# Group attention: the low part of the probabilities two slots behind the scores, four probability buffers, and the half product ahead of the jobs in each slot

## The chip, the cores and the metric

The kernel runs on one core of one Trainium2 chip, in one launch. The metric is the device time of a run in microseconds (us); the kernel before takes 2767.14 us, the median of three runs (2764.65 to 2774.29).

## The reference, cut to what matters

One decoder layer on x of shape (2, 512, 512): causal self-attention with 16 heads, then a grouped attention, then an expert layer with 8 experts. Each adds to x after a layer norm. The change lies in the second part:

```python
q  = _ln(fp8_linear(ln_out, wq)  ...)          # 8 groups x 2 heads, head size 128
k  = _ln(fp8_linear(ln_out, wk)  ...); v = fp8_linear(ln_out, wv)
core = softmax(q  @ k.T  / sqrt(128)) @ v      # 512 keys: x itself
qx = _ln(fp8_linear(ln_out, wqx) ...)
xout = softmax(qx @ kx.T / sqrt(128)) @ vx     # 1024 keys: the context
catq = to_fp8(concat([core, xout]) / proj_smooth)
x = x + (catq @ wproj.T) * (proj_in_scale * proj_w_scale)
```

The output has to agree with a float32 computation, so a float32 operand of a matrix product is kept as two float16 parts, high and low, and a product is three matmuls: high by high, high by low, low by high.

## The kernel before, in words

The group attention (`group_attention`, lines 1189 to 1691) works through 16 steps, one for each of 8 groups and 2 batches (`STEPS`). A step has 16 slots, numbered u = 0 to 15. A slot is one block of 128 queries by all keys of one kind. Slots 0 to 7 are self slots (two heads, four blocks each, 512 keys, scores of 128x512); slots 8 to 15 are cross slots (1024 keys, 128x1024). The steps are written out for the first and the last group, and are the body of a hardware loop over the six groups between: two steps in each pass.

Every engine has a queue of its own, written out slot by slot, and waits on counters (semaphores) that the others raise. For unit u (the work that begins in slot u) the chain is:

- TensorE, `scores`: three or six matmuls into one of two PSUM buffers, `SC[u % 2]`. It waits until the exponential of unit u-2 has read that buffer.
- VectorE, `maxima` (line 1513): the negated row maximum.
- ScalarE, `exp` (line 1430): exp(score - max) into `prob[u % 2]`, float32, with its row sum. It waits for the maximum, and until `parts_lo` of unit u-2 has read the buffer.
- VectorE, `reciprocal` (lines 1517 and 1519): the factor from the row sum of unit u-1, in slot u.
- ScalarE, `parts_hi` (line 1438): prob times the factor, as float16, of unit u-1, in slot u, right after the exponential of unit u.
- VectorE, `parts_lo` (line 1525): prob times the factor minus the high part, as float16. Before, this is unit u-1 in slot u, and the last thing VectorE does in the slot.
- SyncE, `turn` (line 1278): a DMA transpose of both parts into `pt[u % 8]`.
- TensorE, `product`: values times turned probabilities of a pair of units, in two halves. It runs LAG = 6 slots behind: in slot u, the half number u % 2 of the pair that begins with unit u-6 (or u-7). The first half waits until both units of the pair have landed.

Beside this chain a slot has jobs (`SLOT_JOBS`): A0 to A3 (slots 0 to 3) and B0, B1 (4, 5) project queries, keys and values of the next step; Y0 to Y3 (8 to 11) are the output projection of the step before; T4 (12), T0 (13), T1 (14), T2 and T3 (15) turn the normalised queries and keys of the next step. TensorE runs the job after `scores` and, before the change, ahead of `product`. ScalarE reads an A, B or T job at the end of the same slot (`read_job`), after `exp` and `parts_hi`. VectorE takes up what the job gives in the next slot. Jobs use two PSUM banks by turns, and a job waits until the one before it in its bank has been read: T1 for T4, T3 for T1.

An output of attention is read by ScalarE (`output`, line 1446, in slots 2, 6, 10, 14), rounded to float8 by VectorE in four short operations (`output_round`, lines 850 to 856, in slots 3, 6, 11, 15) and finished by GpSimd (`quantised`, line 1348, into `cat`). The job Y0 waits for all four kinds of the step before; the last of them is read and rounded in slot 6 and finished in slot 7. GpSimd also splits the weights of coming groups (lines 1297 to 1304) and, from slot 7, normalises the queries and keys that the T jobs turn (lines 1316 to 1333).

Of the kernel before, what the change touches and what calls it, by code (L numbers as in the profile page):

```python
# [15 lines left out]
ALU = mybir.AluOpType  # L16
ACT = mybir.ActivationFunctionType
AX = mybir.AxisListType
F32 = mybir.dt.float32
# [5 lines left out]
P = 128  # L25
B, S, D = 2, 512, 512
# [40 lines left out]
def after(eng, sem, count):  # L67

    if not isinstance(count, int) or count > 0:
        eng.wait_ge(sem, count)  # L70
# [754 lines left out]
SX = 1024  # L825
# [4 lines left out]
UX = KINDS * BT  # L830
SELF_U = HPG * BT
SLOTS = 8
PARTS_KEPT = 4
LAG = 6
P_SCALE = 2.0 ** 15
# [348 lines left out]
def landings(n, u):  # L1184

    return 16 * (UX // SLOTS * n + u // SLOTS + 1)


def group_attention(nc, ins, sem, sb, bank, X, ident, cols, rcols, xq, kv_d, gw, rows3):


# [4 lines left out]
    STEPS = GROUPS * B  # L1196
# [11 lines left out]
    kv = [sb(f"xkv{b}", [P, KV], F16) for b in range(B)]  # L1208
    kxh, kxl = ([kv[b][:, SX * i:SX * (i + 1)] for b in range(B)] for i in range(2))
    vxh, vxl = ([kv[b][:, SX * i:SX * (i + 1)].rearrange("p (t c) -> p t c", t=XT) for b in range(B)] for i in (2, 3))  # L1210
    prob = [sb(f"xprob{i}", [P, SX], F32) for i in range(2)]
    parts = [sb(f"xparts{i}", [P, 2 * SX], F16) for i in range(PARTS_KEPT)]
    pt = sb("xpt", [P, SLOTS, 2 * XT, P], F16)
    nm, rs, ri = (sb(f"x{x}", [P, 4], F32) for x in ("nm", "rs", "ri"))
    rr = sb("xrr", [P, 1], F32)
    hcols = sb("hcols", [P, 8], F32)
    y, unit, total = sb("xy", [P, S], BF16), sb("xunit", [P, S], BF16), sb("xtotal", [P, S], BF16)
    cat = sb("cat", [P, KINDS, S], F16)
# [2 lines left out]
    SC = [bank[:, 2 * i:2 * i + 2, :].rearrange("p a c -> p (a c)") for i in range(2)]  # L1221
# [47 lines left out]
    with nc.Block() as block:  # L1269
# [115 lines left out]
        def _(act):  # L1385
# [40 lines left out]
            def exp(n, u):  # L1426
                L = S if u < SELF_U else SX
                act.wait_ge(maxed, UX * n + u + 1)
                after(act, lo, UX * n + u - 1)
                act.activation(prob[u % 2][:, 0:L], SC[u % 2][:, 0:L], ACT.Exp,  # L1430
                               bias=nm[:, u % 4:u % 4 + 1], accum_out=rs[:, u % 4:u % 4 + 1]).then_inc(exped, 1)

            def parts_hi(n, u):

                L = S if u < SELF_U else SX
                act.wait_ge(recip, UX * n + u + 1)
                after(act, landed[(u - PARTS_KEPT) % SLOTS], landings(n, u - PARTS_KEPT))
                act.activation(parts[u % PARTS_KEPT][:, 0:L], prob[u % 2][:, 0:L], ACT.Copy,  # L1438
                               scale=ri[:, u % 4:u % 4 + 1]).then_inc(hi, 1)

            def output(n, kind):
# [44 lines left out]
        def _(dve):  # L1486
# [27 lines left out]

            def reciprocal(n, u):
                dve.wait_ge(exped, UX * n + u + 1)
                dve.reciprocal(rr[:], rs[:, u % 4:u % 4 + 1]).then_inc(inverted, 1)
                dve.wait_ge(inverted, UX * n + u + 1)
                dve.tensor_scalar(ri[:, u % 4:u % 4 + 1], rr[:], P_SCALE, None, ALU.mult).then_inc(recip, 1)  # L1519

            def parts_lo(n, u):
                L = S if u < SELF_U else SX
                dve.wait_ge(hi, UX * n + u + 1)
                part = parts[u % PARTS_KEPT]
                dve.scalar_tensor_tensor(out=part[:, L:2 * L], in0=prob[u % 2][:, 0:L],  # L1525
                                         scalar=ri[:, u % 4:u % 4 + 1], in1=part[:, 0:L], op0=ALU.mult,
                                         op1=ALU.subtract).then_inc(lo, 1)

# [24 lines left out]
            def step(g, n, b, first, last, last_group):  # L1553
                for u in range(UX):
                    maxima(n, u)
                    if not (first and u == 0):
                        reciprocal(n if u else n - 1, (u - 1) % UX)
                    for name in SLOT_JOBS.get(u - 1, ()):
                        if name[0] == "Y" and not first:
                            project_out(n - 1, int(name[1]), 1 - b)  # L1560
                        if name in V_ORDER and not last:
                            value_lo(name, n + 1, 1 - b)
                        if name[0] in "AB" and not last:
                            block_stats(name, n + 1)
                    if u in ROUND_AT and not (first and u < LAG + 2):
                        output_round(n if u >= LAG + 2 else n - 1, ROUND_AT[u])
                    if u == 7 and b == 0:

                        after(dve, o_read, KINDS * n)
                        dve.tensor_copy(rsm[:], rcols[:, bass.ds(C_SMOOTH + KINDS * g, KINDS)]).then_inc(s_rsm, 1)  # L1570
                    if not (first and u == 0):
                        parts_lo(n if u else n - 1, (u - 1) % UX)

            def body(g, first, last):
                step(g, 2 * g, 0, first, False, last)
# [1 line left out]

            loop(body)(dve)
            reciprocal(STEPS - 1, UX - 1)
            parts_lo(STEPS - 1, UX - 1)  # L1580
            output_round(STEPS - 1, 2)
            output_round(STEPS - 1, 3)
# [6 lines left out]
        def _(pe):  # L1589
# [44 lines left out]
            def scores(n, u, b):  # L1634
                kind, qt = u // BT, u % BT
                after(pe, exped, UX * n + u - 1)
                tok = slice(P * qt, P * (qt + 1))
                q, l = qh[b][:, kind, tok], ql[b][:, kind, tok]
                a, c = (kh[b], kl[b]) if u < SELF_U else (kxh[b], kxl[b])
                for j in range(1 if u < SELF_U else 2):  # L1640
                    r = slice(S * j, S * (j + 1))
                    last = three(pe, SC[u % 2][:, r], q, l, a[:, r], c[:, r], True, True)
                last.then_inc(scored, 1)
# [23 lines left out]
            def step(g, n, b, first, first_before, last):  # L1667
                for u in range(UX):
                    if u % BT == 0:
                        pe.wait_ge(t_lo, len(T_ORDER) * n + 2 + u // BT)  # L1670
                    if u == SELF_U:
                        pe.wait_ge(kv_in[b], 16 * (g + 1))
                    scores(n, u, b)
                    for name in SLOT_JOBS.get(u, ()):
                        if name in jobs_of(first, last):
                            if b == 1 and name == "A0":
                                pe.wait_ge(w_lo, w_base(g) + W1N)
                            if b == 1 and name == "B0":
                                pe.wait_ge(w_lo, w_base(g) + W1N + W2N)
                            if b == 1 and name == "Y0":  # L1680
                                pe.wait_ge(w_lo, w_base(g) + (W3N if last else WN))
                            run_job(name, n + 1, 1 - b, jobs_of(first, last), NEXT if first else jobs_of(first_before, False))
                    if not (first and u < LAG):
                        product(n if u >= LAG else n - 1, (u - LAG) % UX // 2, b if u >= LAG else 1 - b, u % 2)

            def body(g, first, last):
                step(g, 2 * g, 0, first, False, False)
# [313 lines left out]
```

## Time and profile before

| | us |
|---|---|
| median of three runs | 2767.14 (2764.65 to 2774.29) |
| the profiled execution | 2769.0 |
| its span, first to last instruction | 2767.2 |
| TensorE matmuls busy | 2398.0 (87%) |
| VectorE busy | 1413.4 (51%) |
| ScalarE busy | 1124.9 (41%) |
| GpSimd busy | 1138.1 (41%) |

The mean granted TensorE clock is 0.930 of full speed. A line of a timeline gives the start and length of an instruction or of several alike, its engine, its line in the kernel, its operation, the tiles that it writes and reads, their shapes and count, and in brackets how long the engine had been idle before it and for whom it waited. Matmuls are pipelined: one can be shown as running while the next has begun, so the time that one takes is the distance between two starts. The group attention lies between about 563 and 1745 us of the span; the expert layer follows.

### The profile page before, as it was taken

The numbers are of one execution on the slowest core, as the hardware profiler recorded it, in microseconds if no ns is written. First come the engines' busy times: TensorE is split into PE (matmuls) and PEld (weight loads), VectorE is DVE, ScalarE is ACT, GpSimd is POOL, SyncE is SP. The second block draws the span as 40 slices with busy tenths as digits, with TensorE's granted clock in tenths as the row PEclk, the third lists the DMA queues.
The fourth block names the chain that finished last, engine by engine and source line by source line (L and its number), as shares of the span: only waits on it lengthen the run. The fifth ranks groups of instructions, "written<-read, shape, count | busy, mean of one in ns | idle before, by whom it ended". The sixth has DMA issues, their size and how long they took to land. (4 is left out here: it accounts for less than half of the span.)

```text
span 2767.2 us, 42142 instructions
## 1 busy us (share of the span) xinstructions
PE 2398.0 (87%) x14528; PEld 1338.6 (48%) x14528; DVE 1413.4 (51%) x2920; ACT 1124.9 (41%) x2101; POOL 1138.1 (41%) x1476
## 2 busy tenths in 40 slices
PE   6899899768877878788878876699999999999999
PEld 4566444435555555455545543344444444444444
DVE  5766784347776767676767765522222122322221
ACT  3455464456665656565556653211111111111110
POOL 3322266476565646464637450332231313132231
PEclk9899799889998989898989998799999999999999
DMA  3100022245656566666566564302011110102000
GB/s 136 44 17 5 16 92 107 92 107 107 145 107 133 108 130 112 108 122 125 118 124 122 107 126 80 152 31 92 31 61 53 38 61 30 61 30 91 0 0 30
DMA packets 421584, 225.03 MB, mean 81 GB/s; under 512 B 404400, under 2 KB 404912, under 8 KB 413232
## 3 DMA queue, kind: packets, MB, share of 16 engines
q1 hardware_dynamic: 415952, 186.74, 29.5%
q10 hardware_dynamic: 5472, 36.18, 3.8%
q8 instruction: 97, 1.59, 0.2%
q14 instruction: 63, 0.52, 0.1%
HBM read 103.34 MB, written 18.87 MB: 44 GB/s over the span
## 5 line engine op out<-in xcount | busy, mean ns | idle before, releaser
L1430 ACT ACTIVATE xprob<-bank,xnm 128x512 f32<-128x512 f32 (+1 forms) x256 | 230.7, 901 | 460.4 <-DVE xnm L1513 460.3
L1525 DVE SCALAR_TENSOR_TENSOR xparts<-xprob,xri,xparts 128x512 f16<-128x512 f32 (+1 forms) x256 | 288.5, 1127 | 238.3 <-ACT xparts L1438 237.6
L1804 ACT ACTIVATE sil<-bank 128x512 f32<-128x512 f32 x128 | 76.4, 597 | 772.4 <-PE bank L299 772.4
L1777 POOL TENSOR_SCALAR hh<-h 128x512 f16<-128x512 f32 x128 | 105.1, 821 | 679.0 <-DVE h L1875 678.8
L1875 DVE TENSOR_TENSOR h<-bank,sil 128x512 f32<-128x512 f32 x128 | 88.6, 692 | 530.6 <-PE bank L299 423.2
L1513 DVE TENSOR_REDUCE xnm<-bank 128x1 f32<-128x512 f32 (+1 forms) x256 | 243.6, 952 | 95.5 <-PE bank L299 94.6
L1438 ACT ACTIVATE xparts<-xprob,xri 128x512 f16<-128x512 f32 (+1 forms) x256 | 236.3, 923 | 1.9 <-DVE xri L1519 1.9
L297 PE MATMUL bank<-eXTh,ewh_gate 128*128 128x512 f16 x512 | 194.8, 380 | 4.3 <-DVE ewl_gate L1822 4.3
L298 PE MATMUL bank<-eXTh,ewl_gate 128*128 128x512 f16 x512 | 194.6, 380 | 0.0
L299 PE MATMUL bank<-eXTl,ewh_gate 128*128 128x512 f16 x512 | 194.6, 380 | 0.0
L297 PE MATMUL bank<-eXTh,ewh_up 128*128 128x512 f16 x512 | 194.1, 379 | 0.3 <-DVE ewl_up L1822 0.3
L298 PE MATMUL bank<-eXTh,ewl_up 128*128 128x512 f16 x512 | 194.0, 379 | 0.0
L299 PE MATMUL bank<-eXTl,ewh_up 128*128 128x512 f16 x512 | 194.0, 379 | 0.0
L297 PE MATMUL bank<-ewh_down,hh 128*128 128x512 f16 x512 | 194.0, 379 | 0.0
L298 PE MATMUL bank<-ewh_down,hl 128*128 128x512 f16 x512 | 194.0, 379 | 0.0
L299 PE MATMUL bank<-ewl_down,hh 128*128 128x512 f16 x512 | 194.0, 379 | 0.0
L1625 PE MATMUL bank<-ident,qr 128*128 128x128 f32 x320 | 63.2, 330 | 140.7 <-ACT ft L1423 83.7
L1348 POOL TENSOR_TENSOR cat<-xtotal,xunit 128x512 f16<-128x512 bf16 x64 | 84.0, 1312 | 234.7 <-DVE xtotal L856 234.7
L1333 POOL TENSOR_SCALAR qr<-qr,xrstd,xshift 128x128 f32<-128x128 f32 x320 | 168.9, 545 | 3.1 <-POOL xshift L1328 2.7
L1779 POOL TENSOR_TENSOR hl<-h,hh 128x512 f16<-128x512 f32 x128 | 153.3, 1198 | 21.9 <-POOL hh L1777 20.5
L297 PE MATMUL bank<-xpt,xkv 128*128 128x256 f16 x512 | 151.5, 296 | 9.5 <-DMA xpt<-xparts 9.5
L1630 PE MATMUL bank<-xw3h,cat 128*128 128x512 f16 x256 | 106.6, 416 | 60.9 <-POOL cat L1348 57.2
(259 smaller groups left out, 6034.2 us busy)
## 6 DMA issues: line engine op xcount, KB each, us to landing
xkv<-kv_made ACTq DMA_DIRECT2D x16, 1024.0 KB, 6.5
raw_gate<-in_gate SPq DMA_DIRECT2D x8, 2048.0 KB, 8.0
raw_up<-in_up SPq DMA_DIRECT2D x8, 2048.0 KB, 8.0
raw_down<-in_down SPq DMA_DIRECT2D x8, 2048.0 KB, 8.1
xwraw<-in_w_group ACTq DMA_DIRECT2D x15, 1024.0 KB, 5.2
kv_made<-vst SPq DMA_DIRECT2D x16, 512.0 KB, 4.2
kv_made<-kst SPq DMA_DIRECT2D x16, 512.0 KB, 2.6
kvraw<-in_w_kvx SPq DMA_DIRECT2D x4, 1024.0 KB, 6.5
```

The source lines that it names most:

```text
L297: pe.matmul(ps, ah, bh, start=start, stop=False)
L298: pe.matmul(ps, al, bh, start=False, stop=False)
L299: return pe.matmul(ps, ah, bl, start=False, stop=stop)
L1333: pool.tensor_scalar(norm_block(i), norm_block(i), rstd[:, i:i + 1], shift[:, i:i + 1], ALU.mult, ALU.add)\
L1430: act.activation(prob[u % 2][:, 0:L], SC[u % 2][:, 0:L], ACT.Exp, bias=nm[:, u % 4:u % 4 + 1], accum_out=rs[:, u % 4:u % 4 + 1]).then_inc( ...
L1438: act.activation(parts[u % PARTS_KEPT][:, 0:L], prob[u % 2][:, 0:L], ACT.Copy, scale=ri[:, u % 4:u % 4 + 1]).then_inc(hi, 1)
L1513: dve.tensor_reduce(nm[:, s:s + 1], SC[u % 2][:, 0:L], AX.X, ALU.max, negate=True).then_inc(maxed, 1)
L1525: dve.scalar_tensor_tensor(out=part[:, L:2 * L], in0=prob[u % 2][:, 0:L], scalar=ri[:, u % 4:u % 4 + 1], in1=part[:, 0:L], op0=ALU.mult, o ...
L1630: pe.matmul(J, c, w3h[:, kind, :], start=(kind == 0), stop=False)
L1777: pool.tensor_scalar(hh[half][:, f, :], h[i % 2][:], 1.0, 1.0, ALU.mult, ALU.mult).then_inc(h_hi, 1)
L1779: pool.tensor_tensor(hl[half][:, f, :], h[i % 2][:], hh[half][:, f, :], ALU.subtract).then_inc(h_lo, 1)
L1875: dve.tensor_tensor(h[i % 2][:], bank[:, 2 * (i % 2) + 1, :], sil[i % 2][:], ALU.mult).then_inc(made, 1)
```

## The change: what it does

`parts_lo` of unit u-2, not u-1, runs in slot u, and its place in VectorE's queue is right after `reciprocal`, ahead of the jobs and the rounding. The exponential of unit u would then overwrite a buffer still to be read, so there are four probability buffers and not two: three of 1024 columns that units 1 to 15 take in turn, and one of 512 columns for unit 0. The exponential of unit u waits for `parts_lo` of the unit that had its buffer before: u-3 for u above 3, and units 13, 14, 15 of the step before for u = 1, 2, 3. The reciprocal's scratch gets four columns. On TensorE `product` moves ahead of the jobs in each slot.

```diff
+def prob_of(u):
+    return (u - 1) % 3 if u else 3
+
+def prob_user(u):
+    return u - 3 if u > 3 else u - 4 if u else -UX
...
-    prob = [sb(f"xprob{i}", [P, SX], F32) for i in range(2)]
+    prob = [sb(f"xprob{i}", [P, SX], F32) for i in range(3)] + [sb("xprob_s", [P, S], F32)]
...
-                after(act, lo, UX * n + u - 1)
-                act.activation(prob[u % 2][:, 0:L], SC[u % 2][:, 0:L], ACT.Exp,
+                after(act, lo, UX * n + prob_user(u) + 1)
+                act.activation(prob[prob_of(u)][:, 0:L], SC[u % 2][:, 0:L], ACT.Exp,
...
                     maxima(n, u)
                     if not (first and u == 0):
                         reciprocal(n if u else n - 1, (u - 1) % UX)
+                    if not (first and u < 2):
+                        parts_lo(n if u >= 2 else n - 1, (u - 2) % UX)
                     for name in SLOT_JOBS.get(u - 1, ()):
...
-                    if not (first and u == 0):
-                        parts_lo(n if u else n - 1, (u - 1) % UX)
...
             reciprocal(STEPS - 1, UX - 1)
+            parts_lo(STEPS - 1, UX - 2)
             parts_lo(STEPS - 1, UX - 1)
...
                     scores(n, u, b)
+                    if not (first and u < LAG):
+                        product(n if u >= LAG else n - 1, (u - LAG) % UX // 2, b if u >= LAG else 1 - b, u % 2)
                     for name in SLOT_JOBS.get(u, ()):
...
-                    if not (first and u < LAG):
-                        product(n if u >= LAG else n - 1, (u - LAG) % UX // 2, b if u >= LAG else 1 - b, u % 2)
```

## Rows read from the trace of the kernel before

**Rows 1.** Busy times: page; middle steps (PE, PEld, DVE, ACT, POOL, clock, DMA share, GB/s).
```profile
PE 2398.0 (87%) x14528; PEld 1338.6 (48%) x14528; DVE 1413.4 (51%) x2920; ACT 1124.9 (41%) x2101; POOL 1138.1 (41%) x1476
...
637.90:1644.10 1006.20, 802.99 (x5546) 532.61 (x5545) 704.27 (x1492) 594.63 (x1038) 566.95 (x811) 0.91 0.61 120
```

**Rows 2.** Timeline of VectorE, cross slots 11 to 13 of step 7.
```profile
1114.60 0.28 DVE L850 TENSOR_SCALAR xy<-xy 128x512 bf16<-128x512 bf16 x1
...
1116.08 1.28 DVE L1525 SCALAR_TENSOR_TENSOR xparts<-xprob,xri,xparts 128x1024 f16<-128x1024 f32 x1
1117.28 1.22 DVE L1513 TENSOR_REDUCE xnm<-bank 128x1 f32<-128x1024 f32 x1
...
1118.67 0.74 DVE L1507 SCALAR_TENSOR_TENSOR X<-bank,psc,X 128x512 f32<-128x512 f32 x1
1120.81 1.28 DVE L1525 SCALAR_TENSOR_TENSOR xparts<-xprob,xri,xparts 128x1024 f16<-128x1024 f32 x1 [1.40 <-ACT xparts L1438]
1122.01 1.22 DVE L1513 TENSOR_REDUCE xnm<-bank 128x1 f32<-128x1024 f32 x1
```

**Rows 3.** Timeline of ScalarE, slots 12 and 14 of step 7.
```profile
1118.53 1.11 ACT L1430 ACTIVATE xprob<-bank,xnm 128x1024 f32<-128x1024 f32 x1 [2.49 <-DVE xnm L1513]
...
1119.64 1.14 ACT L1438 ACTIVATE xparts<-xprob,xri 128x1024 f16<-128x1024 f32 x1
1120.67 0.77 ACT L1421 ACTIVATE xkh<-bank,hcols 128x512 f16<-128x512 f32 x1
1121.34 0.77 ACT L1423 ACTIVATE ft<-bank,hcols 128x512 f32<-128x512 f32 x1
...
1130.13 0.68 ACT L1446 ACTIVATE xy<-bank,rsm 128x512 bf16<-128x512 f32 x1
```

**Rows 4.** Timeline of TensorE, cross slots 9 and 15 of step 7.
```profile
1104.90 0.38 PE L297 MATMUL bank<-xkv,xqh 128*128 128x512 f16 x1
...
1106.20 0.38 PE L1630 MATMUL bank<-xw3h,cat 128*128 128x512 f16 x1
...
1107.92 0.27 PE L297 MATMUL bank<-xpt,xvh 128*128 128x256 f16 x1
...
1108.58 0.38 PE L297 MATMUL bank<-xkv,xqh 128*128 128x512 f16 x1
...
1132.27 1.11 PE L1625 MATMUL bank<-ident,qr 128*128 128x128 f32 x4 [4.65 <-ACT ft L1423]
```

**Rows 5.** Timeline of TensorE, self slots 1 and 2 of step 8: starts of scores.
```profile
1146.66 0.38 PE L297 MATMUL bank<-xkh,xqh 128*128 128x512 f16 x1
...
1150.37 0.38 PE L297 MATMUL bank<-xkh,xqh 128*128 128x512 f16 x1
```

**Rows 6.** Timeline of VectorE: slots 6 and 9 of step 8, slot 0 of step 9.
```profile
1166.11 0.69 DVE L1513 TENSOR_REDUCE xnm<-bank 128x1 f32<-128x512 f32 x1 [0.42 <-PE bank L299]
...
1168.84 0.52 DVE L850 TENSOR_SCALAR xy<-xy 128x512 bf16<-128x512 bf16 x1 [0.96 <-ACT xy L1446]
...
1180.73 1.23 DVE L1513 TENSOR_REDUCE xnm<-bank 128x1 f32<-128x1024 f32 x1 [1.32 <-PE bank L299]
...
1214.66 0.69 DVE L1513 TENSOR_REDUCE xnm<-bank 128x1 f32<-128x512 f32 x1 [0.52 <-PE bank L299]
```

**Rows 7.** Timeline of GpSimd and of TensorE, slots 7 and 8 of step 8.
```profile
1172.31 1.49 POOL L1348 TENSOR_TENSOR cat<-xtotal,xunit 128x512 f16<-128x512 bf16 x1 [0.79 <-DVE xtotal L856]
...
1173.94 0.58 PE L1630 MATMUL bank<-xw3h,cat 128*128 128x512 f16 x1 [4.62 <-POOL cat L1348]
```

**Rows 8.** Timeline of TensorE: first scores of step 8, first in a pass of the loop.
```profile
1140.30 0.61 PE L297 MATMUL bank<-xkh,xqh 128*128 128x512 f16 x1 [4.50 <-issue]
```

**Rows 9.** The tile xpt: DMA transposes, from issue to landing.
```profile
DMA to landing us min/median/max: 3.0/4.2/9.5
```

**Rows 10.** Timeline of VectorE: a low part of 512 columns while GpSimd splits weights.
```profile
1086.76 1.74 DVE L1525 SCALAR_TENSOR_TENSOR xparts<-xprob,xri,xparts 128x512 f16<-128x512 f32 x1 [0.38 <-ACT xparts L1438]
...
1090.55 0.75 DVE L1525 SCALAR_TENSOR_TENSOR xparts<-xprob,xri,xparts 128x512 f16<-128x512 f32 x1 [0.38 <-ACT xparts L1438]
```

More of the change, by code:

```diff
@@ L1210, in group_attention @@
     vxh, vxl = ([kv[b][:, SX * i:SX * (i + 1)].rearrange("p (t c) -> p t c", t=XT) for b in range(B)] for i in (2, 3))
-    prob = [sb(f"xprob{i}", [P, SX], F32) for i in range(2)]
+    prob = [sb(f"xprob{i}", [P, SX], F32) for i in range(3)] + [sb("xprob_s", [P, S], F32)]
     parts = [sb(f"xparts{i}", [P, 2 * SX], F16) for i in range(PARTS_KEPT)]
     pt = sb("xpt", [P, SLOTS, 2 * XT, P], F16)
-    nm, rs, ri = (sb(f"x{x}", [P, 4], F32) for x in ("nm", "rs", "ri"))
-    rr = sb("xrr", [P, 1], F32)
+    nm, rs, rr, ri = (sb(f"x{x}", [P, 4], F32) for x in ("nm", "rs", "rr", "ri"))
     hcols = sb("hcols", [P, 8], F32)
@@ L1437, in parts_hi @@
                 after(act, landed[(u - PARTS_KEPT) % SLOTS], landings(n, u - PARTS_KEPT))
-                act.activation(parts[u % PARTS_KEPT][:, 0:L], prob[u % 2][:, 0:L], ACT.Copy,
+                act.activation(parts[u % PARTS_KEPT][:, 0:L], prob[prob_of(u)][:, 0:L], ACT.Copy,
                                scale=ri[:, u % 4:u % 4 + 1]).then_inc(hi, 1)
@@ L1516, in reciprocal @@
                 dve.wait_ge(exped, UX * n + u + 1)
-                dve.reciprocal(rr[:], rs[:, u % 4:u % 4 + 1]).then_inc(inverted, 1)
+                dve.reciprocal(rr[:, u % 4:u % 4 + 1], rs[:, u % 4:u % 4 + 1]).then_inc(inverted, 1)
                 dve.wait_ge(inverted, UX * n + u + 1)
-                dve.tensor_scalar(ri[:, u % 4:u % 4 + 1], rr[:], P_SCALE, None, ALU.mult).then_inc(recip, 1)
+                dve.tensor_scalar(ri[:, u % 4:u % 4 + 1], rr[:, u % 4:u % 4 + 1], P_SCALE, None, ALU.mult).then_inc(recip, 1)
             def parts_lo(n, u):
@@ L1524, in parts_lo @@
                 part = parts[u % PARTS_KEPT]
-                dve.scalar_tensor_tensor(out=part[:, L:2 * L], in0=prob[u % 2][:, 0:L],
+                dve.scalar_tensor_tensor(out=part[:, L:2 * L], in0=prob[prob_of(u)][:, 0:L],
                                          scalar=ri[:, u % 4:u % 4 + 1], in1=part[:, 0:L], op0=ALU.mult,
```

## The prediction

> **What bounds the kernel now.** I read the page's busy times first, then the busy times of the group attention, then the timelines of its engines slot by slot, and last the landings of the transposes. TensorE is busy for 87% of the span, VectorE for 51% [rows 1]: the reader is to see that this average hides a stage in which it is not so. In the 14 middle steps of the group attention, 1006.2 us in all and so 71.9 us a step, TensorE is busy for 80% at a granted clock of 0.91, VectorE for 70%, ScalarE for 59% [rows 1]. Nobody is full, so a chain of waits sets the pace, and the timelines show which. In the cross slots maximum follows maximum every 4.73 us (1117.28 and 1122.01) [rows 2]. The links: maximum at 1117.28, exponential at 1118.53, high part at 1119.64, low part at 1120.81, which VectorE has awaited for 1.40 us, next maximum at 1122.01 [rows 2, 3]. They are one after the other on two engines: 1.25 + 1.11 + 1.17 + 1.20 = 4.73. TensorE would need only 3.68 us for the slot with the costliest job (scores 1.30, job 1.72, half product 0.66) [rows 4]. In the self slots with A and B jobs it is the other way: scores follow every 3.71 us and TensorE is never idle [rows 5]; no gain lies there. Between, slots 6 to 8 hang on the last rounding: in step 8, from the maximum of slot 6 at 1166.11, the rounding begins 2.73 us later, because VectorE waits 0.96 us for the output; cat is written at 1172.31 and Y0 can start at 1173.94, after TensorE has idled for 4.62 us [rows 6, 7].
>
> **The low part, a slot later.** When VectorE reaches the low part of unit u-2, the high part has long been written: ScalarE did it right after the exponential of u-1. The wait of 1.40 us goes, and the ring of 4.73 us is open: maximum, exponential, high part no longer come back to the next maximum. The number of operations stays, and no engine gets more work. What is late next has to be worked out for each stretch; I take step 8 as the pattern.
>
> *Slots 9 to 15.* Before: from 1180.73 to 1214.66, 33.9 us [rows 6]. After, from the maximum of slot 9: slots 9 and 10 go at TensorE's 3.68 each, 7.4. In slot 11 VectorE has maximum and reciprocal 1.39, low part 1.20, projection 0.66 (it had 0.74 at most) and rounding 1.48 (1114.60 to 1116.08) [rows 2]: 4.7, at 12.1. From there ScalarE is the slowest: its exponential of slot 12 starts 1.25 later, at 13.4, and a slot with a T job costs it 1.11 + 1.03 + two reads of 0.67, 3.48 [rows 3]. Slots 12 and 13 take 7.0, slot 14 with an output of 0.6 takes 4.1, so the read of T1 ends at 24.4. T3 waits for that read, as it waited 4.65 us before; it took 1.11 us there [rows 4], I take 0.6 at full clock, then self scores of 0.65 (half of the 1.30): 25.7, the maximum of slot 0. Gain 8.2 us a step. Check by busy time: VectorE has seven times (1.39 + 1.20) and four projections and two roundings, 23.7 us, under the 25.7.
>
> *Slots 6 to 8.* Before: from 1166.11 to 1180.73, 14.6 us [rows 6]. The start of the rounding does not move (the output comes after the same three operations of ScalarE); the low part of unit 4 fills the 0.96 us that VectorE waited. So cat and Y0 stay at 7.8 us behind the maximum of slot 6. But TensorE now has slot 8's half product behind it (0.66), and VectorE's low part no longer stands ahead of the maxima of 7 to 9; what is left is Y0 and the scores of 9, 3.0 us, at 10.9 us. It can be 13.9 if TensorE runs at half clock: before, Y0's first matmul took 0.58 us after 4.62 us of idling, where one of its kind takes 0.38 when TensorE comes out of work [rows 4, 7]: that is the lower of its two levels, 1.2 GHz. The idling that remains is 3.9 us. I take 12.1, a gain of 2.5; both ends are kept, 0.7 and 3.7.
>
> *Slots 0 to 5.* TensorE sets the pace before and after, 3.7 us each [rows 5]. ScalarE now enters slot 0 some 3 us behind, with T2 and T3 to read, and A0 waits for its bank: I charge 0.4 us a step. The pause of 4.50 us at the head of each pass of the loop is TensorE's own [rows 8] and stays.
>
> **The half product ahead of the jobs.** Nothing is added; the same matmuls swap places. The product is ready 0.5 to 1.8 us earlier, the job that much later. Behind an A or B job stand ScalarE's reads, which must end before the next exponential: in a slot of 3.71 us the job ends 0.65 + 1.3 us of product and 1.7 of job after the scores begin, the reads take less than a T job's 1.34 (the blocks are smaller), and the next exponential is due one maximum, 0.7, after the next scores end. That leaves room in a slot of 3.71, so I cost it at nothing; without the room it would be up to 0.5 us in six slots, 3 us a step. In the T slots its 0.66 to 1.3 us is hidden behind ScalarE's work, which is longer.
>
> **The transposes.** Each low part, and so its DMA, is issued most of a slot later, and the product stands earlier. The pair waited for in slot u+6 has its second low part in slot u+3: three slots of 3.7 us less 2.1 to 2.6 us from maximum to low part, 8.5 to 9 us. Landing takes 3.0 to 9.5 us, median 4.2 [rows 9]. The long ones stand beside the weight loads. Bounds: nothing, or 2 us at two pairs of a step. I take 0.5 us a step. The four buffers add no wait: the low part awaited by an exponential (u-3) stands ahead of a maximum that it awaits anyway.
>
> **The low part beside GpSimd.** With GpSimd splitting weights, a low part of 512 columns took 1.74 us instead of 0.75 [rows 10]. It now stands elsewhere in the slot, so other low parts will be stretched. In the TensorE-bound slots this is hidden; in slot 11 and slots 3 to 7 it is not always. Bounds: 1 us gained or 1 us lost each step; I take 0.3 lost. The Trainium skill, GPSIMD Engine Reference, key points, says that GpSimd shares its SBUF interfaces with VectorE, in contention with VectorE instructions that have two SBUF inputs; by that rule each low part beside GpSimd's work could be hit; the trace agrees in the first of the two rows, and what it would add is the end of 1 us above.
>
> **The sum.** A middle step gains 8.2 + 2.5 - 0.4 - 0.5 - 0.3 = 9.5 us, 14 of them 133 us. The first and the last step have fewer jobs, so the ring also sets the pace in their self slots: I estimate 12 us each, 24 in all, from the 9.5 and some 2.5 more for those slots. Together 157 us: 2769.0 - 157 = 2612.0 for an execution like the profiled one, 0.07% above the median of the runs, so some 2610 as a median. Everything outside the group attention is untouched.
>
> **The rivals.**
> 1. *ScalarE and the T jobs keep the old pace in slots 12 to 15.* For it: ScalarE's queue is in order, and the T jobs come after the product and feed reads that stand ahead of the next exponential. Against it: its work there is 3.5 us a slot, not 4.7. Then slots 9 to 11 gain 1.0 each, and slots 6 to 8 the 2.5, less 1.2: 4.3 us a step, 16 steps, 69 us: 2698.
> 2. *Everything falls well.* No stretch, no late landing, Y0 at full clock, ends of 16 us: 8.2 + 3.7 - 0.4 = 11.5, by 14, plus 32: 193 us, 2574.
> 3. *TensorE is the bound already*, and the change does nothing: 2767. For it the 87%, against it the idle 20% in the steps [rows 1] and the 4.73 against 3.68. [...]
> 4. *Slower: TensorE stalls on landings.* The half product now stands ahead of the job, with the pair's low part a slot later; if a landing comes over some 9 us after the issue, TensorE stands still with the job behind it, and after an idle time like that of [rows 7] works on at 1.2 GHz. A wait of 4 us costs 4 plus some 2.7 (5.5 us of work at half clock). One or two such pairs a step eat the gain; at three, 20 - 9.5 = 10.5 us a step is lost, 16 steps, 168 us: 2935. Against it: the median landing of 4.2 us, and that each step has few loads.
>
> **How the numbers follow.** Forecast 0.62, rival 1 0.22, rival 2 0.10, rival 3 0.02, rival 4 0.04. The likeliest gives 2610. Its own range is 2575 to 2655. The 80% range takes in rival 1 and its neighbourhood, 2565 to 2700. What this measurement can tell from no change is some 0.3%, 8 us. Faster: 0.94; within: 0.02; slower: 0.04.
>
> **What would show it.** In the new trace VectorE's low part should wait for ScalarE almost nowhere (before, 1.40 us in such a slot), cross slots 9 and 10 should be 3.7 us apart, slots 12 to 14 some 3.5 to 4.1, with ScalarE waiting little for the maximum there; T3 should still wait for the read of T1, for 2 to 3 us; self slots stay at 3.7. Steps should be near 62 us, and the granted clock of the stage rise. It is wrong if cross slots stay above 4.5 us, or if TensorE is seen to wait for the transposes (xpt) by more than 1 us a step, or for ScalarE in slots 0 to 5.

## The result and the profile after

The changed kernel takes 2628.53 us (median of four runs, 2618.21 to 2643.95) against 2767.27 (four runs, 2764.65 to 2774.29): a ratio of 0.950, 95% interval 0.945 to 0.955. That is 139 us less, where 157 were forecast. The profiled execution took 2629.77 us, its span 2628.0.

The busy times of the whole kernel and of its 14 middle steps (columns as in [rows 1]):

```profile
PE 2340.2 (89%) x14528; PEld 1319.2 (50%) x14528; DVE 1411.5 (54%) x2920; ACT 1124.8 (43%) x2101; POOL 1170.1 (45%) x1476
...
626.90:1518.60 891.70, 750.37 (x5548) 514.57 (x5547) 701.58 (x1492) 593.85 (x1036) 598.56 (x810) 0.95 0.71 135
```

The middle steps fell from 1006.2 to 891.7 us, 63.7 a step. VectorE's busy time is the same (704 before), TensorE's is lower by 53 us for the same matmuls: less of it runs at the lower clock, 0.95 granted against 0.91.

From the starts of the maxima (line 1513 before, 1522 after), us per step. Where the turn of the loop or a step in which GpSimd splits weights matters, they stand apart:

| stretch | before | forecast | after |
|---|---|---|---|
| slots 0 to 5, even / odd steps | 23.8 / 23.6 | 0.4 more | 23.6 / 23.2 |
| slots 6 to 8, even steps (with weight split) | 13.8 | 2.5 less | 13.7 |
| slots 6 to 8, odd steps | 11.4 | 2.5 less | 8.8 |
| slots 9 to 15, without the turn | 34.1 | 8.2 less | 26.2 |
| what the turn adds to slot 15 | 5.0 | same | 7.7 |
| step 0 / 15 slots of step 15 | 62.4 / 59.6 | 12 less each | 50.9 / 46.9 |

(After, slots 9 to 15 of even steps without step 8, which is told of below.)

The new cross slots, on the timeline of VectorE, steps 6 and 7: slots 9 and 10 start 3.67 us apart, and the low part of 1024 columns stands in the middle of the slot and waits for nobody.

```profile
980.12 1.23 DVE L1522 TENSOR_REDUCE xnm<-bank 128x1 f32<-128x1024 f32 x1 [3.08 <-PE bank L299]
983.79 1.23 DVE L1522 TENSOR_REDUCE xnm<-bank 128x1 f32<-128x1024 f32 x1 [0.87 <-PE bank L299]
...
998.27 1.22 DVE L1522 TENSOR_REDUCE xnm<-bank 128x1 f32<-128x1024 f32 x1
...
999.66 1.90 DVE L1534 SCALAR_TENSOR_TENSOR xparts<-xprob,xri,xparts 128x1024 f16<-128x1024 f32 x1
1001.49 1.21 DVE L1522 TENSOR_REDUCE xnm<-bank 128x1 f32<-128x1024 f32 x1
...
1002.90 1.28 DVE L1534 SCALAR_TENSOR_TENSOR xparts<-xprob,xri,xparts 128x1024 f16<-128x1024 f32 x1
...
1005.08 1.32 DVE L856 TENSOR_TENSOR xtotal<-xy,xunit 128x512 bf16<-128x512 bf16 x1
1006.33 0.68 DVE L1522 TENSOR_REDUCE xnm<-bank 128x1 f32<-128x512 f32 x1
```

From the waits of the whole kernel (engine, line, tile waited for: us in total, times, longest), the wait that the change was to remove, and the waits for transposes. Of these, 7.0 us of TensorE and 7.3 us of ScalarE fall in slot 12 of step 8, the rest in the first and the last step:

```profile
DVE xparts L1534 <- ACT xparts L1447: 6.1, 3, 4.6
...
PE bank L297 <- DMA xpt<-xparts: 22.8, 7, 7.0
ACT xparts L1447 <- DMA xpt<-xparts: 10.1, 2, 7.3
```

The busy times of slots 11 to 15 of step 6 show what paces them now (window; then PE, PEld, DVE, ACT, POOL):

```profile
987.47:1006.33 18.86, 14.83 (x100) 9.72 (x99) 18.48 (x31) 15.28 (x23) 11.66 (x15) 1.00 0.87 155
```

VectorE is busy for 18.5 of 18.9 us. ScalarE, which the forecast had named from slot 12 on, is busy for less in this window, but from the exponential of slot 12 to the read of T1, for which T3 waits, its queue has no pause either:

```profile
993.69 1.11 ACT L1439 ACTIVATE xprob<-bank,xnm 128x1024 f32<-128x1024 f32 x1 [2.72 <-DVE xnm L1522]
...
997.16 1.11 ACT L1439 ACTIVATE xprob<-bank,xnm 128x1024 f32<-128x1024 f32 x1
...
1003.97 0.81 ACT L1432 ACTIVATE ft<-bank,hcols 128x512 f32<-128x512 f32 x1
...
1004.92 0.65 PE L1635 MATMUL bank<-ident,qr 128*128 128x128 f32 x4 [2.28 <-ACT ft L1432]
```

Slots 7 and 8 of step 6, on GpSimd and TensorE, answer to [rows 7], and the turn of the loop into step 8 to [rows 8], with T3 ahead of it:

```profile
973.17 1.15 POOL L1357 TENSOR_TENSOR cat<-xtotal,xunit 128x512 f16<-128x512 bf16 x1 [0.79 <-DVE xtotal L856]
...
974.46 0.59 PE L1640 MATMUL bank<-xw3h,cat 128*128 128x512 f16 x1 [4.26 <-POOL cat L1357]
...
1063.16 0.65 PE L1635 MATMUL bank<-ident,qr 128*128 128x128 f32 x4 [2.18 <-ACT ft L1432]
1070.80 0.61 PE L297 MATMUL bank<-xkh,xqh 128*128 128x512 f16 x1 [6.99 <-issue]
```

Landings ([rows 9] before):

```profile
DMA to landing us min/median/max: 3.0/4.3/20.0
```

### The profile page after: what moved, and what is told of

The parts are those of the page before. It is cut to its first block and busy times, and to the rows that moved or that the text cites. A ratio compares the mean times of both kernels' runs of the same rounds, so it can differ in the third digit from the quotient of the medians.

```text
span 2628.0 us, 42146 instructions
## 1 busy us (share of the span) xinstructions
PE 2340.2 (89%) x14528; PEld 1319.2 (50%) x14528; DVE 1411.5 (54%) x2920; ACT 1124.8 (43%) x2101; POOL 1170.1 (45%) x1476
## 5 line engine op out<-in xcount | busy, mean ns | idle before, releaser
L1439 ACT ACTIVATE xprob<-bank,xnm 128x1024 f32<-128x1024 f32 (+1 forms) x240 | 221.1, 921 | 231.9 <-DVE xnm L1522 231.8
L1534 DVE SCALAR_TENSOR_TENSOR xparts<-xprob,xri,xparts 128x1024 f16<-128x1024 f32 (+1 forms) x240 | 275.4, 1148 | 6.1 <-ACT xparts L1447 6.1
L1447 ACT ACTIVATE xparts<-xprob,xri 128x1024 f16<-128x1024 f32 (+1 forms) x240 | 227.4, 947 | 10.7 <-DMA xpt<-xparts 10.1
L1342 POOL TENSOR_SCALAR qr<-qr,xrstd,xshift 128x128 f32<-128x128 f32 x320 | 181.8, 582 | 3.1 <-POOL xshift L1337 2.7
L1895 DVE SCALAR_TENSOR_TENSOR X<-bank,wcol,X 128x512 f32<-128x512 f32 x64 | 48.0, 751 | 214.4 <-PE bank L299 214.4
L1357 POOL TENSOR_TENSOR cat<-xtotal,xunit 128x512 f16<-128x512 bf16 x64 | 73.6, 1150 | 200.2 <-DVE xtotal L856 200.2
L297 PE MATMUL bank<-xpt,xkv 128*128 128x256 f16 x512 | 143.5, 280 | 9.3 <-DMA xpt<-xparts 9.3
L298 PE MATMUL bank<-xpt,xkv 128*128 128x256 f16 x512 | 143.6, 280 | 0.0
```

The lines of the kernel that those rows point to most:

```text
L297: pe.matmul(ps, ah, bh, start=start, stop=False)
L298: pe.matmul(ps, al, bh, start=False, stop=False)
L1342: pool.tensor_scalar(norm_block(i), norm_block(i), rstd[:, i:i + 1], shift[:, i:i + 1], ALU.mult, ALU.add)\
L1439: act.activation(prob[prob_of(u)][:, 0:L], SC[u % 2][:, 0:L], ACT.Exp, bias=nm[:, u % 4:u % 4 + 1], accum_out=rs[:, u % 4:u % 4 + 1]).then ...
L1447: act.activation(parts[u % PARTS_KEPT][:, 0:L], prob[prob_of(u)][:, 0:L], ACT.Copy, scale=ri[:, u % 4:u % 4 + 1]).then_inc(hi, 1)
L1534: dve.scalar_tensor_tensor(out=part[:, L:2 * L], in0=prob[prob_of(u)][:, 0:L], scalar=ri[:, u % 4:u % 4 + 1], in1=part[:, 0:L], op0=ALU.mu ...
```

## The experiments

Each ratio is to the kernel before, run on the same chip, with its 95% interval; the medians are of five runs, six for the second. Differences to the changed kernel are differences of medians to 2628.6 us, its repeat below; from the fifth experiment on they go across chips, and by the ratios they come out up to 4 us different.

**VectorE's part alone.** The changed kernel, with TensorE's order as before:

```diff
                     scores(n, u, b)
-                    if not (first and u < LAG):
-                        product(...)
                     for name in SLOT_JOBS.get(u, ()):
                         ...
+                    if not (first and u < LAG):
+                        product(...)
```

> VectorE's part of the change alone (low part two slots behind, right after the reciprocal, four buffers); on TensorE the half product stays behind the jobs, as before. Theory A (the ring maximum, exponential, high part, low part was what paced the cross slots, and VectorE's move alone opens it): the whole gain is here. The changed kernel came to 2628.5 us; without the product ahead of the jobs the loop's turn should cost TensorE what it did before (some 5.0 us a pass and not 7.7, five passes, 13 us), and Y0's slots some 0.65 us each more where they are late: 2610 to 2625 us. Cross slots 9 and 10 at 3.7 us. Rival B (the order on TensorE carries part of the gain, because a product behind the job holds up landings, buffers or the clock): 2660 to 2700 us.

Measured: 2665.09 us, 0.9638 (0.9622 to 0.9654). 99 us below before and 36 above the changed kernel: in the range of rival B. Cross slots 9 and 10 are at 3.68 us, so the ring does open by VectorE's move alone. The rest is lost mostly at four places. Against the repeat of the changed kernel the 14 middle steps of the profiled execution take 42 us more: 15 in slot 15 (where no turn follows it takes 7.6 us in four steps of nine and 5.5 to 7.9 in the others, instead of 4.8), 17 in slot 12, where three steps wait 5.4 to 8.1 us for a transpose, 12 in slot 13 and 7 in slot 8, while slot 0 gives 8 back. From the waits:

```profile
PE bank L297 <- DMA xpt<-xparts: 29.9, 9, 7.2
...
ACT xparts L1447 <- DMA xpt<-xparts: 27.4, 7, 8.1
PEld bank L297 <- DMA xpt<-xparts: 18.7, 3, 7.4
```

**TensorE's part alone.** The kernel before, with the `product` lines moved ahead of the jobs.

> TensorE's part alone: the half product ahead of the jobs in each slot, VectorE and the two buffers as before. Theory A: the ring of 4.73 us stays in slots 9 to 14, so nothing is gained there, and the product no longer covers the loop's turn: 2767 to 2785 us, the step through the loop's turn longer by 2 to 3 us. Rival B (the order carries part of the gain): 2700 to 2740 us.

Measured: 2746.55 us, 0.9934 (0.9919 to 0.995). The ring stays, as theory A has it: low parts 4.73 us apart, each after a wait for the high part.

```profile
1114.21 1.28 DVE L1525 SCALAR_TENSOR_TENSOR xparts<-xprob,xri,xparts 128x1024 f16<-128x1024 f32 x1 [2.05 <-ACT xparts L1438]
...
1118.94 1.28 DVE L1525 SCALAR_TENSOR_TENSOR xparts<-xprob,xri,xparts 128x1024 f16<-128x1024 f32 x1 [2.05 <-ACT xparts L1438]
```

But the order is worth 18 us, against both theories. In the middle steps of the profiled execution slot 15 gives 8.5 us (where no turn follows it takes the ring's 4.73 us instead of 5.1 to 5.8), and slots 0 to 3 together give 11. 99 and 18 make 117; the remaining 19 of the 136 appear only when both are done.

**The product last in slot 15 alone, and the changed kernel again.**

```diff
-                    if not (first and u < LAG):
+                    if u != UX - 1 and not (first and u < LAG):
                         product(...)
                     for name in SLOT_JOBS.get(u, ()):
                         ...
+                    if u == UX - 1:
+                        product(...)
```

> The changed kernel with one slot put back: in slot 15 the half product stands behind T2 and T3 again, in all others ahead of the jobs. Theory A (after the branch TensorE's next matmul comes 7.6 us later, in both kernels, and only what is queued behind the last wait covers it; the product of slot 15 was that cover): the five steps that end at the loop's turn get shorter by 2.5 us, 12 us in all, and the other steps stay: 2613 to 2620 us against 2628. Rival B (the longer pause has another cause, the turn meets ScalarE later): no change, 2625 to 2632 us, pause after T3 still 7.2 us.

> The changed kernel again, unchanged, for a comparison on the same chip, and to see whether the late landing of the profiled execution (slot 12 of step 8 took 10.6 us and not 3.2) comes again. If it was one late transfer, no step has it or another one has; if it is the place in the program, step 8 has it again. Both: 2618 to 2640 us.

Measured: 2653.43 us, 0.9589 (0.9573 to 0.9605), and 2628.63 us, 0.9513 (0.9499 to 0.9526). My theory fell: putting back one slot of sixteen costs 25 us. Before I ran it I had read the longer pause at the turn as lost cover. The timelines of TensorE in slot 15 of step 10 tell what happens. With the product last, TensorE idles 3.40 us before T3, and from there on T3, the product and the next scores all run at the lower clock:

```profile
1286.92 1.11 PE L1635 MATMUL bank<-ident,qr 128*128 128x128 f32 x4 [3.40 <-ACT ft L1432]
1287.83 0.42 PE L297 MATMUL bank<-xpt,xkv 128*128 128x256 f16 x1
...
1290.38 0.63 PE L297 MATMUL bank<-xkh,xqh 128*128 128x512 f16 x1
```

With it ahead (the changed kernel again), the product runs in that idle time, 2.28 us are left, and the clock stays at its upper level:

```profile
1262.14 0.27 PE L299 MATMUL bank<-xpt,xkv 128*128 128x256 f16 x1
1262.25 0.60 PE L1635 MATMUL bank<-ident,qr 128*128 128x128 f32 x4
1265.13 0.65 PE L1635 MATMUL bank<-ident,qr 128*128 128x128 f32 x4 [2.28 <-ACT ft L1432]
1265.62 0.38 PE L297 MATMUL bank<-xkh,xqh 128*128 128x512 f16 x1
```

From T3 to the scores it is 3.46 us against 0.49, and slot 15 takes 8.4 us against 4.8. Of these 3.6 us, 1.3 are the product's own time (1260.94 to 1262.25 with the product ahead), moved out of the wait, and 2.3 are what the lower clock adds to T3, the product and the scores. The Trainium skill, TensorE: Matmul & The Clock Gate, "What's actually happening", says that the default state is throttled and that activity releases it; these two timelines agree, at 0.42 against 0.27 us for the same matmul.

At the turn the same experiment shows that the pause is no fixed cost behind the last matmul. In the turn into step 8, with the product last, the pause is 4.09 us, shorter as expected, but from T3 to the first scores it is 7.76 us; in the changed kernel 7.64, before 8.03 ([rows 4, 8]: 1132.27 to 1140.30). Over the five turns of each profiled execution it is 7.8 to 8.4 us before, 7.5 to 8.9 in the two of the changed kernel, and 7.7 to 9.0 with the product last.

```profile
1078.62 1.11 PE L1635 MATMUL bank<-ident,qr 128*128 128x128 f32 x4 [3.39 <-ACT ft L1432]
1086.38 0.61 PE L297 MATMUL bank<-xkh,xqh 128*128 128x512 f16 x1 [4.09 <-issue]
```

So what counts is when T3 is let go: 0.8 us after the maximum of slot 15 before, 3.3 after the change. What TensorE does in these 7.5 to 9.0 us no run shows. The late landing did not come again in the second execution of the changed kernel, but it came in the same slot 12 of step 8 in two others, with the product last (8.0 us for the slot) and in the ninth experiment (8.3).

**The low part at the end of the slot.** `parts_lo(u - 2)` moved behind the jobs and the rounding on VectorE.

> The changed kernel with the low part still two slots behind, but at the end of VectorE's slot, behind the jobs and the rounding, where the kernel before had it. Theory A (the distance of two slots opens the ring, the place in the slot matters little): the order of VectorE's work in a slot sums up to the same, cross slots 9 and 10 stay at 3.68 us; in slot 6 VectorE idles before the rounding again, and transposes are issued 1 to 2 us later, so that some more landings are late: 2628 to 2650 us. Rival B (the place carries the gain): 2680 us or more, cross slots above 4 us.

Measured: 2631.66 us, 0.9527 (0.9506 to 0.9547). Theory A: the distance carries the gain, the place in the slot next to nothing. Slot 6 of the odd steps is back at 4.7 us (4.05 in the changed kernel), and TensorE waits for transposes 22 times, 22.5 us in all (6 times, 16.0 us, in the repeat of the changed kernel). No run has the four buffers without the distance. Before, `parts_lo` of unit u-2 stood ahead of `maxima` of unit u in VectorE's queue, so an exponential that waited for its maximum [rows 3] had nothing left to wait for at its buffer.

**The weights scaled a slot earlier.** In even steps, on GpSimd:

```diff
                 for u in range(UX):
+                    if b == 0 and u == 3 and not last_group:
+                        scale_raw(1, 2 * g + 1)
                     if u in QUANTISED_AT and not (first and QUANTISED_AT[u][1]):
                         quantised(...)
                     if b == 0 and u == 4 and not last_group:
                         split(1, ...)    # without the scalings
```

> The changed kernel with one thing moved on GpSimd: in even steps the eight scalings of the coming group's query weights run in slot 3, ahead of cat of kind 2, and not behind it; the split follows as before, so it ends some 4 us earlier. Theory A (slots 6 to 8 of even steps are paced by the last rounding, which takes 3.3 us and not 1.4 because GpSimd splits weights beside it, and TensorE then runs at half clock after waiting for cat): slot 6 falls from 6.58 to 4.05 us and slot 8 from 5.2 to 2.9, as in the odd steps, 4.8 us in six steps, 29 us: 2598 to 2605 us. Rival B (the rounding is slow for another cause, or the earlier scalings hold up kind 2 and with it the rounding): 2620 to 2640 us.

Measured: 2603.15 us, 0.9423 (0.9401 to 0.9446), 25 us below the changed kernel. Theory A in place and nearly in size: slots 6 to 8 of the six even steps fall from 13.7 to 10.1 us. In step 4 Y0 is let go after 2.22 us and runs at the upper clock:

```profile
833.76 0.43 DVE L856 TENSOR_TENSOR xtotal<-xy,xunit 128x512 bf16<-128x512 bf16 x1
...
834.37 1.15 POOL L1364 TENSOR_TENSOR cat<-xtotal,xunit 128x512 f16<-128x512 bf16 x1 [2.83 <-DVE xtotal L856]
...
835.66 0.38 PE L1649 MATMUL bank<-xw3h,cat 128*128 128x512 f16 x1 [2.22 <-POOL cat L1364]
```

So it is in three of the six steps, where slot 8 takes 2.8 us. In steps 6, 10 and 12 Y0 also starts at the upper clock, after nearly the same idle time, but the clock falls behind its first matmuls, and slot 8 takes 4.5. That is what the gain lacks of the 29 us; step 6:

```profile
961.02 0.38 PE L1649 MATMUL bank<-xw3h,cat 128*128 128x512 f16 x1 [2.19 <-POOL cat L1364]
...
961.95 0.63 PE L1650 MATMUL bank<-xw3l,cat 128*128 128x512 f16 x1
```

**The T jobs one slot earlier.**

```diff
-             10: ("Y2",), 11: ("Y3",), 12: ("T4",), 13: ("T0",), 14: ("T1",), 15: ("T2", "T3")}
+             10: ("Y2",), 11: ("Y3", "T4"), 12: ("T0",), 13: ("T1",), 14: ("T2",), 15: ("T3",)}
```

> The changed kernel with the T jobs one slot earlier: T4 behind Y3 in slot 11, T0, T1, T2, T3 in slots 12 to 15, one in each. Theory A (from slot 12 on ScalarE's reads set the pace, and T3 waits for the read of T1): VectorE paces slot 11 anyway (5.0 us), so T4's read is free there; slot 15 falls from 4.8 to about 2.6 to 3.2 us, the wait of 2.3 us ahead of T3 goes, and the turn of the loop begins earlier by as much. 2 us in 14 steps, 28 us, and up to 5 more at the turns: 2595 to 2605 us. Rival B (VectorE or TensorE sets the pace there as well): 2620 to 2630 us. Rival C (GpSimd has not normalised the blocks in time for T4 in slot 11, and TensorE waits for it): slot 11 grows, 2630 us or more.

Measured: 2655.04 us, 0.9601 (0.9579 to 0.9623), 26 us worse. The time is in rival C's range and slot 11 grows (5.0 to 5.5 us), but the cause is none of my theories. T4 and T0 use the banks of Y2 and Y3, and VectorE adds those to x a slot later. TensorE stands at T0 for 2.88 us in step 8, and slot 12 takes 7.1 us instead of 3.2. From the waits, and the timeline of TensorE:

```profile
PE bank L1635 <- DVE X L1516: 46.7, 19, 3.4
```

```profile
1132.64 0.65 PE L1635 MATMUL bank<-ident,qr 128*128 128x128 f32 x4 [1.13 <-DVE X L1516]
...
1138.12 0.99 PE L1635 MATMUL bank<-ident,qr 128*128 128x128 f32 x4 [2.88 <-DVE X L1516]
```

**The context load later.** In even steps `load_kv(g, 1, ...)` in slot 12 instead of slot 8.

> The changed kernel with the load of the context's keys and values (1 MB) in even steps issued in slot 12 and not in slot 8, right behind the load of 1 MB of weights. Theory A (transposes that land late, up to 12.9 to 20.7 us after their issue, are those issued beside these two loads, and the slack for them is one slot smaller than before the change): no more waits of TensorE or ScalarE for a transpose in slots 12 and 13 of even steps, and the longest landing falls; 0 to 8 us off and less spread, 2620 to 2628 us. Rival B (they are late for a cause outside these loads): same median and spread, single slots of 5 to 10 us too long come again.

Measured: 2617.31 us (2615.05 to 2620.78), 0.9472 (0.9452 to 0.9492). The longest landing is 9.4 us, where the two executions of the changed kernel had 20.0 and 12.9:

```profile
DMA to landing us min/median/max: 3.0/4.3/9.4
```

This fits theory A in the landings. In the two later kernels that keep the load in slot 12 the longest is 9.6 and 8.8 us, and in all nine profiled executions that have the change and the load in slot 8 it is 10.9 to 20.7. The 11 us are clear of the noise, but their cause isn't shown: 4 of them lie ahead of the group attention in the profiled executions, where the edit changes nothing, and the tenth experiment doesn't repeat the gain.

**Short second reads on ScalarE.**

```diff
-                    last = act.activation(ft[i % 2][:], J, ACT.Identity, ...)
+                    r = slice(0, S if isinstance(m, int) and m == 0 else 64)
+                    last = act.activation(ft[i % 2][:, r], J[:, r], ACT.Identity, ...)
```

> The changed kernel with less work for ScalarE: of each T job's second read (the float32 copy ft that GpSimd takes the low part from) only 64 of 512 columns are computed, except for the first step; the low parts of queries and keys are left wrong by it. Theory A (from slot 12 on ScalarE's queue, with two reads of 0.67 us for each T job, decides when T3 can start, and with it slot 15 and the turn of the loop): a short read takes some 0.2 us, T3 starts 1.2 to 1.5 us earlier, slot 15 falls from 4.8 to 3.4 us, the step through the turn by as much, and A0 is no longer late in slot 0: 1.3 to 2 us in 15 steps, 2600 to 2610 us. Rival B (VectorE's or TensorE's own work sets the pace there): 2622 to 2632 us.

Measured: 2617.76 us, 0.9462 (0.9447 to 0.9477). Only 11 us, and not where I expected them: slot 0 falls from 4.7 to 3.9 us on average (A0, where it is late, waits 0.4 us for ScalarE and not 0.8), slot 15 stays at 4.86, and slot 13 grows from 2.6 to 3.4, because GpSimd's subtraction now falls beside VectorE's low part. Slots 11 to 15 of its step 10:

```profile
1249.66:1269.53 19.87, 16.02 (x109) 10.55 (x107) 19.49 (x30) 15.91 (x26) 11.92 (x15) 1.00 0.76 142
```

VectorE is busy for 19.5 of 19.9 us, with the low part of slot 13 stretched, where that of slot 15 is not:

```profile
1259.26 2.24 DVE L1536 SCALAR_TENSOR_TENSOR xparts<-xprob,xri,xparts 128x1024 f16<-128x1024 f32 x1
1259.27 1.16 POOL L1350 TENSOR_TENSOR xkl<-ft,xkh 128x512 f16<-128x512 f32 x1 [3.80 <-ACT ft L1433]
...
1266.06 1.27 DVE L1536 SCALAR_TENSOR_TENSOR xparts<-xprob,xri,xparts 128x1024 f16<-128x1024 f32 x1
```

**Both moves that gained, and the first rounding in slot 13.** The second adds to the first `ROUND_AT` 13 for 11 and `QUANTISED_AT` 14 for 13, both for kind 0.

> Both moves that gained, on the changed kernel: the scalings of the query weights in slot 3 (alone 25 us) and the context load of even steps in slot 12 (alone some 11 us). Theory A (they touch different waits: the last rounding in slot 6, and late landings in slots 12 and 13): the gains add up, 2590 to 2597 us. Rival B (the 11 us were the luck of a few transfers): 2600 to 2606 us.

> As e10, and the first rounding of a step (kind 0) moved on VectorE from slot 11 to slot 13, its last operation on GpSimd from slot 13 to 14. Theory A (slot 11 is paced by VectorE with the rounding, 5.0 us where TensorE needs 3.7, and from 12 on ScalarE sets the pace, so that VectorE has room in slot 13): slot 11 falls to 3.7 us, slot 13 grows by 1 to 1.5 us, and of the 1.3 us some 0.5 to 0.9 stay in each of 15 steps: 8 to 13 us less than e10. Rival B (VectorE is as close to its limit in 12 to 15 as ScalarE): the same as e10 or up to 5 us more.

Measured: 2601.34 us, 0.9402 (0.9382 to 0.9421), and 2606.25 us, 0.9437 (0.9411 to 0.9462). The first is the fastest kernel of this study, 27 us below the changed one, but not clear of the scalings alone (0.9423, 0.9401 to 0.9446), nor is theory A's sum reached: rival B is the likelier. In the second slot 11 falls to 3.68 us as expected and slot 13 grows from 2.6 to 4.9, more than expected: VectorE has no room there, which is rival B.

**Short low parts on VectorE.**

```diff
+                c = L if L == S or (isinstance(n, int) and n < 2) else 64
-                dve.scalar_tensor_tensor(out=part[:, L:2 * L], in0=prob[prob_of(u)][:, 0:L], ...
+                dve.scalar_tensor_tensor(out=part[:, L:L + c], in0=prob[prob_of(u)][:, 0:c], ...
```

> The changed kernel with less work for VectorE: the low part of cross units is computed for 64 of 1024 columns from the third step on, the rest is left as an earlier unit left it, so the result is wrong by it. In the changed kernel VectorE is busy for 18.5 of 18.95 us in slots 11 to 15 of step 6, and ScalarE's queue from slot 12 on ends in the same microsecond. Theory A (both bind: VectorE alone in slot 11, VectorE and ScalarE together in 12 to 15; with short reads on ScalarE alone slot 15 did not move): slot 11 falls from 5.0 to 3.7 to 3.9 us, but 12 to 15 together only from 13.9 to about 13.4, what ScalarE's 3.48 + 3.48 + 4.05 and the last turn allow: 1.5 to 2 us in 13 steps, 2600 to 2610 us. Rival B (VectorE alone binds there): slots 12 to 15 fall by another 3 us, 2560 to 2580 us.

Measured: 2615.87 us, 0.9458 (0.9433 to 0.9484). Slots 11 to 15 of step 6:

```profile
987.39:1006.16 18.77, 15.64 (x99) 10.24 (x98) 12.62 (x31) 16.30 (x24) 7.92 (x12) 0.93 0.98 162
```

VectorE is down to 12.6 us, and the stretch is 0.1 us shorter. ScalarE's reads let T3 go at 1003.73, 1.2 us earlier than in the changed kernel's step 6, after an idle time of 3.13 us, and TensorE then works at its lower clock:

```profile
1003.73 1.11 PE L1636 MATMUL bank<-ident,qr 128*128 128x128 f32 x4 [3.13 <-ACT ft L1432]
1004.63 0.63 PE L297 MATMUL bank<-xkh,xqh 128*128 128x512 f16 x1
```

From the exponential of slot 12 to T3 it is 11.2 us in both kernels (992.51 to 1003.73, and 993.69 to 1004.92): ScalarE's queue sets that length, with VectorE at 12.6 us of work as at 18.5, and T3 comes earlier because slot 11 takes 3.9 us instead of 5.0. From T3 to the next maximum it is 2.4 us instead of 1.4. This is theory A, both bind, with the clock taking back 1.0 us of the 1.2. The total came out some 6 us above its range, since the clock's part was not in it.

## Why the prediction was right, and where its steps were off

*The ring of 4.73 us.* Right, in kind and size. VectorE's waits for the high part fell from 237.6 us in all to 6.1, and slots 9 and 10 take TensorE's 3.68.

*Slots 9 to 15.* Right in size, 26.2 against 25.7, and right in the path: in step 6 ScalarE's exponential of slot 12 starts 13.6 us behind the maximum of slot 9 (13.4 forecast), and the read of T1 ends at 24.7 (24.4). Not ScalarE alone bounds the stretch, though, and the step that failed is the check that VectorE had room. I had added up its work at undisturbed lengths and over all seven slots, 23.7 us. In slots 11 to 15 VectorE is busy nearly all the time, because its operations are longer there: beside GpSimd's subtractions a low part takes 1.90 us instead of 1.28 and the last rounding operation 1.32 instead of 0.43. So VectorE and ScalarE end together: in step 6 the scores of slot 0, which follow T3 and so ScalarE's read, are done at 1006.2, and VectorE comes out of the rounding for the maximum at 1006.33. The maxima of slots 12 to 14 came 3.2, 2.6 and 3.2 us apart, not the 3.5 to 4.1 I had named, and slot 15 took 4.8. Relieving either (ninth and twelfth experiment) leaves slots 11 to 15 at 19.9 and 18.8 us where they took 18.9, with 11 and 13 us less in the median, and moving VectorE's work within the stretch gains nothing.

*The low part beside GpSimd.* The term (0.3 us) was right in kind. Inside slots 14 and 15 it is more, 0.6 us for a low part and 0.9 for a rounding operation, and it is contained in the 26.2. It used up VectorE's room more than it lengthened the step.

*The transposes.* The term (0.5 us a step, 7 us in 14) came as a single wait: in slot 12 of step 8 ScalarE and TensorE waited 7.3 and 7.0 us, and the slot took 10.6 us instead of 3.2. The repeat has nothing of that size in its middle steps, so the term belongs to some executions and not to others.

*Slots 6 to 8.* The gain of 2.5 us came in the odd steps (2.6) and not in the even ones in which weights are split (0.1). Step 8, my pattern, was the longest of these before: 14.6 us, where their mean was 13.8 and that of the odd steps 11.4. The step that failed is the middle value of 12.1 for a stretch whose two ends were written down: TensorE still idled 4.26 us ahead of Y0 and came out at its lower clock, so the upper end, 13.9, holds. The sixth experiment shows both causes, the split of the weights beside the rounding and the clock, by taking the first away.

*The half product ahead of the jobs.* Costed at nothing, and it is worth 36 us on top of VectorE's move, 18 without it. The step failed because it looked for a delay of the jobs and not for the idle time that the product could fill: ahead of T3 TensorE has to wait, and what is done in that wait is both free and keeps the clock up. Slot 15 alone, put back, costs 25 us. That doesn't make it 25 of the 36: with every product behind the jobs slot 15 cost 15 us, and most of the rest was lost in slots 12 and 13. My sum had this gain in it all the same, since I worked out the slots with the product ahead.

*The turn of the loop.* Taken as a fixed 4.50 us; it adds 7.7 us to slot 15 instead of 5.0, five times, some 14 us. It runs from T3's release, which ScalarE now gives later in the slot.

*The sum.* Middle steps 114.5 us where 133 were said. The turns gave 14 us less, and slots 6 to 8 gave 22 us instead of 35. Slots 0 to 5 gained 3.5 us where 5.6 were charged, 9 more. Slots 9 to 15 gave 110 us as forecast, and the late landing took the 7 us that the term for transposes had set aside. So the 18 us are two terms put too high, less one put too low. First and last step: 24.2 us for 24. That they did is in part luck, for step 0 waits in slots 12 and 13 and step 15 in slots 1 and 3.

*The signs of being wrong.* Two of those that I had named did show. TensorE waited for ScalarE in slots 0 to 5: A0 in slot 0, 0.8 us in 8 of the 14 middle steps, 6.4 us in all, about the 0.4 us a step that I had charged. And it waited for transposes for 22.8 us in all, over 1 us a step; only 7.0 of them lie in the middle steps, and the repeat has 16.0. Neither overturns the forecast.

What stays open: why transposes land up to 20 us late in some executions beside the loads, and whether the context load's place has a part in the median; and what TensorE does at the turn of the loop.

## What to carry to other kernels

When the distance between the same operations of two slots equals the sum of a chain that goes back and forth between two engines, one slot more between producer and consumer (and one buffer more) frees it, and the gain is the gap to the next engine's own work in that slot. Put independent work ahead of an instruction that has to wait, not behind it; on TensorE the wait so filled also saves the clock. And add up the next engine's load with the lengths that its operations have beside the work of the others, for after such a change two engines easily end in the same microsecond, and relieving one gives little.

## What the runs showed of the hardware

- In most of the slots shown TensorE came out of idle times of 3.13 to 4.65 us at its lower clock (1.2 GHz) and out of those of 2.19 to 2.28 us at its upper one (2.4 GHz): a 128x512 matmul took 0.58 to 0.63 us, or 0.38. The length of the idle time alone doesn't decide. In step 2 of the changed kernel Y0 came out of 4.27 us at the upper clock and lost it after two matmuls of 0.38 us (then 0.47, then 0.63), and in step 6 of the sixth experiment the same happened after 2.19 us, where in step 4, after 2.22, the upper clock stayed.
- From T3, the last wait ahead of the loop's turn, to the first matmul behind the turn TensorE took 7.5 to 9.0 us in 20 turns (the kernel before, the changed one twice, the third experiment), whether or not a product of 12 matmuls stood between.
- A float32 operation of VectorE with two inputs in SBUF (1024 columns, 1.28 us) took 1.90 us (changed kernel) and 2.24 us (ninth experiment) beside subtractions on GpSimd, and a bfloat16 operation with two inputs of 512 columns 1.32 us instead of 0.43. It goes the other way too: in step 6 of the changed kernel a subtraction on GpSimd that began 0.4 us into a low part took 1.92 us instead of 1.15, and the low part its 1.28.
- DMA transposes landed 4.2 to 4.3 us after their issue in the median. With two loads of 1 MB issued in slot 8 of the even steps, the longest landing was 10.9 to 20.7 us in the nine profiled executions that have the change, 9.5 in the kernel before and 12.6 in the second experiment; with one of the loads in slot 12 it was 8.8 to 9.6 in three.
